# Three attentions of a one-core kernel: value projections placed singly, a semaphore of its own for the query weights, queries ahead of the keys in the middle attention

## What is computed

```python
# phase 0 and phase 6: softmax, with biases
q = query @ wq.T + bq; k = ctx @ wk.T + bk; v = ctx @ wv.T + bv     # 16 heads of 16
attn = softmax(q k' / sqrt(16)); x = x + (attn v) @ wo.T + bo
# phase 4: sigmoid in place of the softmax, no biases
scores = sigmoid(q k' * 16 ** -0.5); x = x + (scores v) @ wo.T
```

## Time and profile before

| | |
|---|---|
| median of three runs (lowest to highest) | 2941.83 us (2939.04 to 2946.45) |
| the profiled execution: its time, its span | 2929.89 us, 2928.1 us |
| mean granted TensorE clock | 0.948 of full |
| PE, DVE, ACT, POOL busy | 93%, 56%, 54%, 10% of the span |

### The profile page before, as it was taken

One profiled execution on the slowest core, in us unless ns is written; L12 is line 12 of the kernel. 1 busy time (PEld: TensorE's weight loads), 2 busy tenths in 40 slices (PEclk: granted clock), 3 DMA queues, 4 the chain that ended last, 5 costly groups with the idle time before them and its releaser, 6 DMA issues.

```text
span 2928.1 us, 38798 instructions
## 1 busy us (share of the span) xinstructions
PE 2730.6 (93%) x14644; PEld 1389.7 (47%) x14644; DVE 1629.2 (56%) x2972; ACT 1576.2 (54%) x2681; POOL 307.1 (10%) x256
## 2 busy tenths in 40 slices
PE   7999999999899898999899999979989999999986
PEld 3434334343478766777323333357743343443433
DVE  5777787777374553442111221135667777877844
ACT  1677777777410112110577878932137777777772
POOL 2010100100110101111010110021211001010001
PEclk7899999999899998999899999989979999999997
DMA  5432342330200002000744444220052342333300
GB/s 112 68 38 31 57 53 51 46 41 6 93 1 29 0 1 65 1 1 0 140 54 68 58 67 56 23 90 1 1 67 46 45 68 28 42 57 42 39 1 29
DMA packets 69016, 125.55 MB, mean 43 GB/s; under 512 B 21008, under 2 KB 45528, under 8 KB 65376
## 3 DMA queue, kind: packets, MB, share of 16 engines
q1 hardware_dynamic: 67680, 120.64, 26.9%
q10 hardware_dynamic: 1152, 2.44, 0.3%
HBM read 42.50 MB, written 2.10 MB: 15 GB/s over the span
## 4 chain that ended last, share of the span: by engine, by line
PE 55%; DVE 5%; ACT 2%; issue 2%; SPq 1%; DMA 0%; ACTq 0%; POOL 0%; POOLq 0%; DVEq 0%
PE psum L190 34%; PE psum L707 12%; PE psum L1839 6%; DVE mpart L896 2%; ACT probs L774 2%; SPq L1012 1%; PE psum L278 1%; PE psum L1832 0%; SPq L1013 0%; PE psum L717 0%; DVE prod L1622 0%; PE psum L726 0%; DMA qst<-qp_lo 0%; DVE masked_hi L1926 0%; DVE masked_lo L1927 0%
## 5 line engine op out<-in xcount | busy, mean ns | idle before, releaser
L774 ACT ACTIVATE probs<-psum 128x512 f32<-128x512 f32 (+3 forms) x2080 | 1280.0, 692 | 380.8 <-PE psum L190 379.1
L896 DVE TENSOR_REDUCE mpart<-psum 128x2 f32<-128x804 f32 x1024 | 976.2, 991 | 314.1 <-PE psum L190 304.8
L707 PE MATMUL psum<-probs,vt 128*17 128x512 f32 (+1 forms) x4992 | 668.3, 610 | 1.4 <-ACT probs L774 1.4
L190 PE MATMUL psum<-qst,kst 50*128 50x512 f32 (+3 forms) x2496 | 607.1, 451 | 12.1 <-ACT probs L774 4.8
L190 PEld LDWEIGHTS psum<-qst,kst 50*128 50x128 f32 (+3 forms) x2496 | 269.1, 185 | 414.1 <-issue 260.5
L190 PE MATMUL psum<-kst,qst 48*128 48x402 f32 x2048 | 415.1, 427 | 48.4 <-DVE mpart L896 46.3
L190 PEld LDWEIGHTS psum<-kst,qst 48*128 48x128 f32 x2048 | 197.3, 194 | 358.9 <-issue 179.9
L190 PE MATMUL psum<-wv,ctxT 128*128 128x256 f32 (+1 forms) x624 | 181.6, 419 | 1.5 <-DVE kp_lo L877 0.5
L190 PE MATMUL psum<-ctxT,wk 128*128 128x512 f32 (+1 forms) x384 | 160.1, 547 | 22.8 <-DMA ctxT<-in_ctxT 21.7
L707 PEld LDWEIGHTS psum<-probs,vt 128*17 128x17 f32 (+1 forms) x4992 | 84.8, 96 | 200.7 <-issue 160.1
L190 PEld LDWEIGHTS psum<-wv,ctxT 128*128 128x128 f32 (+1 forms) x624 | 109.8, 194 | 77.9 <-issue 58.5
(11 more groups left out here) (308 smaller groups left out, 2729.1 us busy)
## 6 DMA issues: line engine op xcount, KB each, us to landing
kst<-kp_hi SPq DMA_DIRECT2D x144, 200.1 KB, 5.8
ctxT<-in_ctxT SPq DMA_DIRECT2D x36, 512.0 KB, 4.8
kst<-kp_lo SPq DMA_DIRECT2D x72, 200.1 KB, 5.4
qst<-qp_hi SPq DMA_DIRECT2D x144, 64.0 KB, 4.5
kst<-kp_hi SPq DMA_DIRECT2D x84, 100.1 KB, 2.9
qst<-qp_lo SPq DMA_DIRECT2D x72, 64.0 KB, 5.1
kst<-kp_lo SPq DMA_DIRECT2D x42, 100.1 KB, 3.0
stage<-in_L_ffn_W SPq DMA_DIRECT2D x16, 256.0 KB, 4.5
```

Of the source, the lines that this page charges most:

```text
L190: last = e.matmul(dst, lhsT, rhs, start=i == 0, stop=i == len(pairs) - 1)
L707: t = e.matmul(c.bank(self.acc)[32 * h:32 * h + VW, :], self.vt[0:kn, kc, self.head(g, h), :], p[0:kn, h % self.wide, :], start=kc == 0, s ...
L774: e.activation(self.probs[n % slots][0:kn, :, :], c.psum[0:kn, k:k + self.wide, :], ACT.Exp if softmax else ACT.Sigmoid, scale=DH ** -0.5) ...
L896: e.tensor_reduce(self.mpart[:, :, p * (SEQ // P) + qt, i], c.psum[:, k:k + 2, 0:MAX_WIDTH], AX.X, ALU.max).then_inc(c.drained(k), 1)
```

## The change

It has three parts. In the softmax attentions the seven value steps of the prelude stand singly at -1.11, -0.99, and so on to -0.39: after 3, 7, 11, 15, 19, 23 and 27 of the 32 maxima. The query weights, and their bias, signal a semaphore of their own, bq is issued right behind wq, and the first query step waits for that semaphore alone. In the middle attention wq is loaded ahead of the context, and both query steps stand in front of the first key step, so that half 0 comes behind the fourth key step.

```diff
@@ plan
         put(self.key_steps(0, 0), -3.5, -2.5, prelude)
-        put(self.query_steps(0)[:1], -2.35, -2.3, prelude)
+        if softmax:
+            put(self.query_steps(0)[:1], -2.35, -2.3, prelude)
+            put(self.query_steps(0)[1:], -2.25, -2.2, prelude)
+        else:
+
+            put(self.query_steps(0), -3.6, -3.55, prelude)
         put([("half", f, 0, 0)], -2.28, -2.28)
-        put(self.query_steps(0)[1:], -2.25, -2.2, prelude)
         put(self.key_steps(0, 1), -2, -1.6, prelude)
         put([("half", f, 0, 1)], -1.25, -1.25)
         for i, step in enumerate(self.value_steps(0, 0, 7)):
 
-            at = -1.5 + 0.5 * (i // 3) + 0.01 * (i % 3)
+
+            at = -1.11 + 0.12 * i if softmax else -1.5 + 0.5 * (i // 3) + 0.01 * (i % 3)
             put([step], at, at, first_values)
@@ load
-        self.load_context(e, 0)
-        load_weight(e, self.wq, I[f"{tag}_wq"], w_in)
+        if self.softmax:
+            self.load_context(e, 0)
+        load_weight(e, self.wq, I[f"{tag}_wq"], c.sem(f"{tag}_query_weights_in"))
+        if self.biased:
+            load_columns(e, self.bq, I[f"{tag}_bq"], c.sem(f"{tag}_query_weights_in"))
+        if not self.softmax:
+            self.load_context(e, 0)
         if first:
             for b in range(1, BATCH):
                 load_x(c, e, b)
         load_weight(e, self.wv, I[f"{tag}_wv"], w_in)
         if self.biased:
-            load_columns(e, self.bq, I[f"{tag}_bq"], w_in)
             load_columns(e, self.bv, I[f"{tag}_bv"], w_in)
@@ wait_weights
-        e.wait_ge(self.c.sem(f"{self.tag}_weights_in"), 16 * 6)
+        e.wait_ge(self.c.sem(f"{self.tag}_weights_in"), 16 * (4 if self.biased else 5))
+
+    def wait_query_weights(self, e):
+        e.wait_ge(self.c.sem(f"{self.tag}_query_weights_in"), 32 if self.biased else 16)
@@ tensor, the step "query"
                 if b == cc == 0:
-                    self.wait_weights(e)
+                    self.wait_query_weights(e)
```

## The result

| | before | after |
|---|---|---|
| median of 8 runs each, taken in turn on one chip, us | 2941.09 (2934.36 to 2950.98) | 2951.61 (2946.97 to 2957.45) |
| ratio, 95% interval | | 1.0043 [1.0024, 1.0061] |
| profiled execution: time, span, us | 2929.9, 2928.1 | 2957.45, 2955.7 |
| mean granted clock | 0.948 | 0.936 |

The change makes the kernel slower: the medians are 10.5 us apart, 10.7 were forecast, and 2952.5 was given for 2951.61. The ratio and its interval are estimated from the single runs and are not the quotient of the medians; 1.0043 is 12.6 us, with 7.1 to 17.9 as its interval, which lies clear of no change and takes in the 8.8 us of 0.3%. The two profiled executions are 27.6 us apart. That of before is faster than all eight of its runs here, that of after is the slowest of its eight.

The account below looks back on a forecast made before the run. It took the chain to be mostly PE's, running over DVE's maxima only in the preludes of attentions 0 and 6; -1.25 + 5.4 + 6.3 + 0.2 = +10.65 us, on the median 2941.8 giving 2952.5 us, range 2933 to 2959.

Parts of the forecast that it names:

- Which stage decides: Preludes of attentions 0 and 6: only there the chain runs over DVE's maxima, 59 us, with idle stretches from PE.
- Price and number of the value steps: Softmax preludes: seven single values at 1.64 and 1.63 us of DVE idle, +5.4 us in attention 0, +6.3 in attention 6.
- The clock: Softmax preludes: falls to 1.2 GHz at, or soon after, the first maximum and does not return; all seven values meet it.
- Rival 1: Softmax preludes: clock stays up or returns at once, 0.2 us per value, -9.45 us in all, 2932.4 us; chance 0.13.
- Rival 3: Softmax preludes: maxima hidden by a later wait, half 1 or unit 1 landing late; about -1 us, 2941 us; chance 0.04.
- Rival 2: Softmax preludes: clock oscillates, half of the values meet it full; together +0.6 us, 2942.4 us; chance 0.17.
- What the three values in front cost: Before the first maximum, attentions 0 and 6: three value steps cost DVE nothing, hidden behind ACT's 5.15 us of evacuations.
- The query wait: Attention 0, first query step: wait for wo goes, hT comes last; -1.25 us, bounds 0 and -1.35.
- rival 4: Attention 0, first query step: another wait (hT, bq) replaces the old; +11.9 us, 2953.7 us; chance 0.06.
- Attention 4: Queries before keys: PE starts 0.9 us earlier, first value step +0.2 us; bounds of the part -1.5 and +1.9.
- the bound of up to +1.7 us: Attention 4: if the clock falls in PE's longer wait before the values, 8 values start at half speed.
- The sum: Whole kernel: -1.25 + 5.4 + 6.3 + 0.2 = +10.65 us, added to the median for 2952.5 us; chance 0.60.

Follow-up runs that it names:

- e8: The whole change again, on a second chip, against the kernel before: ratio 1.0039 [1.0023, 1.0054].
- e1: Kernel before with only the seven single value steps in the softmax preludes: ratio 1.0063 [1.0040, 1.0086].
- e2: Kernel before with only the query weights' own semaphore and the earlier bq: ratio 1.0005 [0.9984, 1.0026].
- e3: Kernel before with only attention 4 changed, wq ahead of the context and queries ahead of the keys: ratio 1.0008 [0.9992, 1.0025].
- e4: Kernel before with three value steps kept in front of the first maximum and the other four placed singly: ratio 1.0056 [1.0036, 1.0076].
- e10: Kernel before with DVE's last reduction of the first unit made eight times, a delay without PE work: ratio 1.0023 [1.0002, 1.0044].
- e11: e4 once more on another chip, against the kernel before: ratio 1.0026 [1.0004, 1.0048].
- e6: Kernel before with three value steps in front, four single, and the preludes' maxima matmuls computed three times: ratio 1.0045 [1.0020, 1.0070].
- e5: The change with the matmuls of the preludes' 39 maxima issued twice into the same bank; against the kernel before, ratio 1.0064 [1.0038, 1.0091].
- e9: Kernel before plus query semaphore; softmax values three in front, two after two maxima, two after four, half 1 and unit 1 later: ratio 1.0003 [0.9982, 1.0025].

## Why the prediction was right, and where only in the sum

**Which stage decides.** Right: the losses that come again in all three profiles with single values (the change, e8, e1) are in the two preludes, where DVE waits for PE.

**Price and number of the value steps.** Right: 7 x 1.63 = 11.4 us in each attention; 11.4 less what the earlier trace rows had is +5.3 and +6.3 (forecast +5.4 and +6.3). From first maximum to first probs it is +5.8 and +6.8. The 0.5 us left in each is a small term that the forecast lacked. DVE's reductions in a row come 0.90 us apart (3 take 2.80 us, 4 take 3.70, 16 take 14.53), but one alone takes 1.00; so each break in the row costs 0.1 us beside the idle time. The change has seven breaks in place of two, 0.5 us more, and a single value at 1.2 GHz really costs 1.73 us. From the first maximum to the end of the last of unit 0 the two attentions take 35.26 and 34.24 us before and 41.05 both after, which is the whole +5.8 and +6.8.

**The clock.** Right: it fell within the pause that the move opens, earlier than the forecast's "at, or soon after, the first maximum", and stayed down. But the pause decides less than the forecast gives it: with the three values left in front the clock fell all the same, 1.7 to 8.3 us behind the start of the first maximum in the profiles of before, e2, e3, e4, e10 and e11, and of the four single values of e4 and e11 all but the first met the low clock. What the change lacks is the first maximum at full clock and the return of the clock behind the triple, which in the profile before lasted 3.4 and 6.8 us. Another small term was missing: the first maximum's matmuls now run at 1.2 GHz, 1.04 instead of 0.63 us; from the first query step to the first maximum it takes 0.2 and 0.3 us longer. Rival 1 fell. Its price was right (0.17 us, e4), and e6 shows that its clock can be had, but not from these value steps. Rival 3 fell too: all idle time between the maxima is put down to PE's values, none to half 1. Rival 2 fell with the first: no window of the maxima after the change shows the clock come back. By the rule of the Trainium skill ("TensorE: Matmul & The Clock Gate", section on psum-queue depth-cycling), for a PE that pauses briefly between groups as it cycles through PSUM banks, the clock should alternate; the trace of the change disagrees (0.50 over 47.1 and 41.0 us of maxima), while in e5 the clock did come and go in attention 6 (up for 10.2 us between two low stretches).

**What the three values in front cost.** Right: nothing. ACT still releases the first maximum, which DVE begins at 32.11 us against 32.10. But it was forecast to come 1.2 us earlier (PE at 30.4 instead of 31.6 us) and PE began it at 31.37, because the next term brought next to nothing.

**The query wait.** The term that was mis-sized: -1.25 us, measured -0.2 on the start of the query step between the two profiles and nothing in the median (e2). The step was "with the wait gone hT comes last, and the step starts at about 17.43". hT does come last, but at 17.33 only in the one profile read; in all others but e9 (16.78) it is ready 0.6 to 2.1 us later, near the landing of wo or behind it. The reading behind this, that PE is at full clock until 35.3 us, is wrong for the first keys: they run at half the rate until the clock rises, at 11.4 us in that profile, and in the others up to 3.4 us later behind their start. That was the shortest delay of all thirteen profiles. The forecast's "bounds 0 and -1.35 us" held it, and rival 4, that hT only takes the place of wo, came true in the main.

**Attention 4.** PE's start was forecast 0.9 us earlier and is 0.95 earlier; the first value step +0.2 and is +0.04. Then the bound of up to +1.7 us, should the clock fall there, came true to the tenth (8.00 against 6.31 us), and, in three profiles of four, was the value to take: the text itself said that PE's wait in front grows, and the earlier trace rows show the clock down behind a pause of 2.96 us.

**The sum.** The preludes give +12.8 us in the profile pair (+5.8 and +7.0), where +10.45 was forecast; of the difference the query term accounts for some 1.0, the breaks in DVE's row for 0.9, and the slower first maxima for 0.5. Attention 4 adds +1.7 there. The median gives +10.5, and that this is the forecast's +10.7 is partly luck: the forecast had no term for the units, which were up to 20 us longer in a profile, and the same change with the same preludes cost 10.5 us in one set of runs and 11.3 in another, its value part alone 22.5 in a third, while e4 and e11 lost 17.0 and 7.1 us with preludes at most 1.3 us longer than before. The sign and the mechanism of the preludes are shown; that the median's loss is theirs and nothing else, and the agreement within a microsecond, are not.

## What to carry to other kernels

A step that is moved has a price at each clock. Before spreading work out of a stretch in which TensorE had nothing else to do, ask what it will cost at the clock of its new place: here three hidden value steps became three of 1.63 us of idle time each. The four others cost that much with or without the three in front, but for at most one that came early enough to meet the full clock (0.17 us). A wait read in one profile is worth only what its next releaser leaves; look for the spread of the earlier work in front of it before its length is taken as a gain. And where a kernel spends a tenth of its time at the low clock, a gain of 8 us in one stage need not arrive: time at low clock must be counted over the whole run.

## What was not expected of the hardware

- In e5 PE worked for 44.0 of 47.6 us, for the most part with matmuls of 48 rows, and the granted clock was 0.50 throughout; in attention 6 of the same kernel it was up for 10.2 us. Before the change it rose at 42.1 us, near the end of the three value steps of 128 rows that PE had begun at 37.39.
- The clock fell inside a pause of 3.27 us in both softmax attentions of all four profiles that have one (the change, e8, e1, e5), and 1.0 to 1.4 us behind the end of one of 2.6 to 3.0 us in attention 4; there it stayed up behind one of 1.54 us (e5). It also fell without such a pause, 1.8 us behind the first maximum, in attention 0 of e4.
- Executions of one kernel on one chip differ by up to 41 us (e6: 2929.43 to 2970.15), and the mean clock goes with them, at 0.33 to 0.43 us for each microsecond at 1.2 GHz.
